# The last layer of a four-layer kernel, rewritten from a loop over batches into a written-out pipeline of three stages

## The reference, cut to what matters

```python
xn = _layernorm(x)
# state-space part (HID 512, 64 heads of width 8, N 128, chunks of Q = 128 tokens)
zxbcdt = xn @ W_in.T                      # z 512, channels 512 + 2*128, steps 64
xBC = causal_conv_silu(zxbcdt[512:1280])  # 4 taps
dt = softplus(dt_raw + dt_bias);  a = dt * -exp(A_log)
# within and across chunks: C_i . B_j * exp(sum of a from j to i) * dt_j, times xs_j
y  = (Yd + Yoff) + D * xs
yz = y * silu(z)
yn = yz * rsqrt(mean(yz*yz) + EPS) * norm_w
x  = x + yn @ W_out.T + (sigmoid(xn @ q(w1).T) * (xn @ q(w2).T)) @ q(w3).T
```

## Time and profile before

| What | Value |
|---|---|
| Median of 3 runs | 1151.38 us |
| Profiled execution, its own time | 1151.5 us |
| Its span, first to last instruction | 1149.7 us |
| PE, DVE, ACT, POOL busy | 969.4, 815.7, 449.7, 463.9 us |
| Mean granted clock of TensorE | 0.928 |
| First instruction of layer 3's norm to the end | 681.4 to 1149.7 us |

### The profile page before, as it was taken

One profiled execution on the slowest core, in us unless ns is written; L12 is line 12 of the kernel. 1 busy time (PEld: TensorE's weight loads), 2 busy tenths in 40 slices (PEclk: granted clock), 3 DMA queues, 4 the chain that ended last, 5 costly groups with the idle time before them and its releaser, 6 DMA issues. The chain is left out here.

```text
span 1149.7 us, 13089 instructions
## 1 busy us (share of the span) xinstructions
PE 969.4 (84%) x4130; PEld 500.7 (44%) x4130; DVE 815.7 (71%) x1432; ACT 449.7 (39%) x732; POOL 463.9 (40%) x480
## 2 busy tenths in 40 slices
PE   3888859979999999579999959888988898889777
PEld 1555535523333333235565545325533553355324
DVE  3667655578888786447768737796679767967795
ACT  1111124427766666257536424311442134224421
POOL 2111047555444442025426420681068206910681
PEclk9999979969999999779999978899889988998899
DMA  8500006322222210020000010000000000000000
GB/s 299 181 14 14 14 0 167 109 64 57 57 67 60 70 30 1 25 107 14 1 15 15 1 39 1 1 1 1 18 0 0 0 18 0 0 9 9 0 0 18
DMA packets 28635, 42.95 MB, mean 37 GB/s; under 512 B 6480, under 2 KB 21792, under 8 KB 28192
## 3 DMA queue, kind: packets, MB, share of 16 engines
q1 hardware_dynamic: 28592, 42.41, 11.9%
HBM read 30.93 MB, written 11.27 MB: 37 GB/s over the span
## 5 line engine op out<-in xcount | busy, mean ns | idle before, releaser
L991 DVE TENSOR_REDUCE l_nmax<-banks 128x1 f32<-128x512 f32 (+1 forms) x165 | 147.9, 930 | 35.0 <-PE banks L1094 34.1
L2328 PE MATMUL banks<-l_scaled,l_cbm 128*128 128x512 f32 x224 | 126.9, 687 | 44.1 <-POOL l_scaled L2038 21.2
L950 ACT ACTIVATE l1b_PT<-banks 128x512 f32<-128x512 f32 (+1 forms) x176 | 134.1, 793 | 67.0 <-PE banks L1107 66.6
L2038 POOL TENSOR_TENSOR l_scaled<-l_X,l_source 128x512 f32<-128x512 f32 x112 | 132.6, 1210 | 0.0
L2207 DVE TENSOR_TENSOR banks<-banks,l_decay 128x512 f32<-128x512 f32 x128 | 87.9, 689 | 18.0 <-PE banks L2328 11.0
L2328 PEld LDWEIGHTS banks<-l_scaled,l_cbm 128*128 128x128 f32 x224 | 41.8, 210 | 116.2 <-POOL l_scaled L2038 76.1
L1094 PE MATMUL banks<-l_KQ 96*128 96x512 bf16 x240 | 82.0, 395 | 7.9 <-DVE l_nmax L991 5.0
L1107 PE MATMUL banks<-l_KQ 99*128 99x512 bf16 x256 | 85.7, 388 | 2.8 <-ACT l1b_PT L950 2.1
L2181 DVE TENSOR_TENSOR l_y<-l_y,banks 128x512 f32<-128x512 f32 x128 | 86.5, 676 | 1.9
L2107 ACT ACTIVATE l_hhi<-l_h 128x512 f16<-128x512 f32 (+1 forms) x24 | 15.1, 630 | 144.5 <-DVE l_h L2220 144.5
L1121 PE MATMUL banks<-l1b_PT,l1b_V 128*32 128x512 f32 x512 | 68.2, 605 | 0.0
(11 more groups left out here) (326 smaller groups left out, 2083.6 us busy)
## 6 DMA issues: line engine op xcount, KB each, us to landing
l_split<-l1a_parts SPq DMA_DIRECT2D x16, 384.0 KB, 3.7
l_KQ<-l_split SPq DMA_DIRECT2D x48, 128.0 KB, 2.9
l_KQ<-l_split SPq DMA_DIRECT2D x16, 192.0 KB, 3.0
l_KQ<-l_split SPq DMA_DIRECT2D x48, 64.0 KB, 2.9
w_ternary<-l_tern_out SPq DMA_DIRECT2D x7, 384.0 KB, 2.3
x<-in_x SPq DMA_DIRECT2D x4, 512.0 KB, 9.5
l_raw<-in_w_gate_up SPq DMA_DIRECT2D x2, 1024.0 KB, 10.0
out<-x SPq DMA_DIRECT2D x4, 512.0 KB, 3.0
```

What stands on the lines that cost most here:

```text
L950: nc.scalar.activation(PT[:, first:first + size, :], source, ACT.Exp, scale=SCALE).then_inc(p_ready, 1)
L991: nc.vector.tensor_reduce(nmax[:, H % 2, first:first + size], source, axis=AX.X, op=ALU.max, negate=True).then_inc(smax_read, 1)
L2038: nc.gpsimd.tensor_tensor(by_head(scaled[:, n % 4, :]), by_head(X[:, T, :]), spread(source[:, level, T, :]), ALU.mult).then_inc(scaled_rea ...
L2328: last = nc.tensor.matmul(bank, cbm[:, T % 2, level, :], scaled[:, own_n % 4, :], start=True, stop=True)
```

## The change

Layer 3 is written out for stages b = -1 to 4. In stage b, the 16 units (pairs of tiles, 1,024 columns each) of batch b's products run; at fixed places beside them stand the beginning of batch b + 1 and the projections of batch b - 1. Units 0 to 6 are the levels of tiles 0 and 1, unit 7 is L128, unit 8 is L256, units 9 to 15 are the levels of tiles 2 and 3. A unit is two matmuls into a pair of banks (4,5 or 6,7); banks 0 and 1 serve the feed-forward and the projections, banks 2 and 3 all the rest. `X`, `decay` and `y` get two buffers, `scaled` goes from four of 512 to two of 1,024 columns.

On single parts: dt is multiplied into X once (`start`), in place of the product of decay and dt (L2170). The diagonal of the state product comes from a product of two channel groups on POOL and four matmuls with a column of ones (`sum_states`), in place of L2195 and L2197. The masks of tiles 0 and 1 read PSUM. Normalisation of the input moves from DVE to ACT; y is normalised on ACT before it is turned, so the two output projections accumulate in one bank and two adds into x become one. In layer 1, a memset on POOL moves from ahead of the first inversion to behind the second.

```diff
-            nc.gpsimd.memset(early.KQ[ROWS:ROWS + PARTS, KEY, :, :, :], 1.0).then_inc(early.ones_set, 1)
-            pool.wait_ge(early.ones_set, 1)
             invert(0)
             for b in range(B):
                 add_bias(b)
                 if b + 1 < B:
                     invert(b + 1)
+                if b == 0:
+                    pool.wait_ge(rstd_ready, 2)
+                    nc.gpsimd.memset(early.KQ[ROWS:ROWS + PARTS, KEY, :, :, :], 1.0).then_inc(early.ones_set, 1)
+                    pool.wait_ge(early.ones_set, 1)
...
+            def start(b, half):
...
+                nc.gpsimd.tensor_tensor(by_head(y[:, b % 2, mine, :]), by_head(X[:, b % 2, mine, :]), spread(coef[:, mine, :]),
+                                        ALU.mult).then_inc(y_started, 1)
+                pool.wait_ge(y_started, b * 2 + half + 1)
+                nc.gpsimd.tensor_tensor(by_head(X[:, b % 2, mine, :]), by_head(X[:, b % 2, mine, :]), spread(dt[:, mine, :]),
+                                        ALU.mult).then_inc(xdt_ready, 1)
+
+            def scale(b, n):
...
+                if q >= 2:
+                    pool.wait_ge(prod_made, own_unit(q - 2) + 1)
+                nc.gpsimd.tensor_tensor(by_head(scaled[:, n % 2, :, :]), by_head(X[:, b % 2, mine, :]),
+                                        spread(decay[:, b % 2, level, mine, :]), ALU.mult).then_inc(scaled_ready, 1)
+
+            def scale_across(b, i):
+                pool.wait_ge(xdt_ready, b * 2 + 2)
+                if b:
+                    pool.wait_ge(post_made, b * 2)
...
+                    for n in range(OWN):
+                        scale(b, n)
+                        if n == 2:
+                            rest_of_input(b)
+                        if n == 3 and b:
+                            invert_rms(b - 1)
+                        if n == 5:
+                            scale_across(b, 0)
+                        if n == 6:
+                            scale_across(b, 1)
...
+                        if n == 12 and b + 1 < B:
+                            multiply_states(b + 1)
...
+                if b + 1 < B:
+                    start(b + 1, 0)
+                    start(b + 1, 1)
...
+                for s in range(4, 12):
+                    if ahead and s - 4 < XBC:
+                        take_channels(b + 1, s - 4)
+                    if now and s >= 6:
+                        round_gated(b, s - 6)
+                    if now and 5 <= s < 11:
+                        gate_sigmoid(b, s - 5)
+                    if now and s == 9:
+                        square_tile(b, 0)
+                        square_tile(b, 1)
+                if ahead:
+                    for i in range(CHUNKS):
+                        decays(b + 1, i)
+                    gate_channels(b + 1)
+                    for t in range(TT):
+                        copy_tokens(b + 1, t)
...
+                for u in range(UNITS):
+                    if now:
+                        apply_decay(b, u)
+                    if now and u:
+                        add(b, u - 1)
+                    elif behind and u == 0:
+                        add(b - 1, UNITS - 1)
+                    if behind and u == 0:
+                        gate_y(b - 1, 1)
+                    if u == 1 and behind:
+                        mean_square(b - 1)
+                    if u == 2 and ahead:
+                        copy_turned(b + 1)
+                    if u == 3:
+                        if now:
+                            mask_late(b, 2)
+                            mask_late(b, 3)
+                        if ahead:
+                            take_steps(b + 1)
+                    if u == 4:
+                        if ahead:
+                            softplus(b + 1)
+                        if behind:
+                            add_x(b - 1, 0)
+                    if u == 5 and behind:
+                        add_x(b - 1, 1)
+                    if 5 <= u < 5 + XBC:
+                        if ahead:
+                            convolve(b + 1, u - 5)
+                        if now:
+                            multiply_gate(b, u - 5)
+                    if now and u == ACROSS_128 + 1:
+                        gate_y(b, 0)
...
+                    if u == 12 and ahead:
+                        weigh_skip(b + 1)
+                    if u == 15 and ahead:
+                        mask(b + 1, 0)
+                        mask(b + 1, 1)
...
+            def feed_forward(b, j):
                 rows = P if j < FT - 1 else LAST
-                if j >= 2:
-                    pe.wait_ge(h_ready, b * FT + (j - 1))
+                if j == 0:
+                    pe.wait_ge(split, b + 1)
+                    pe.wait_ge(up_loaded, 16)
+                    if b:
+                        pe.wait_ge(x_done, b * 2)
+                else:
+                    pe.wait_ge(h_ready, b * FT + j)
...
+            def product(b, u):
+                g = b * UNITS + u
+                if g >= 2:
+                    pe.wait_ge(prod_added, g - 1)
+                bank = unit_bank(u)
...
+                    pe.wait_ge(scaled_ready, b * OWN + n + 1)
+                    for i in range(2):
+                        last = nc.tensor.matmul(ps[bank + i][:, :], cbm[:, 2 * (n // LEVELS) + i, n % LEVELS, :],
+                                                scaled[:, n % 2, i, :], start=True, stop=True)
...
+                for u in range(UNITS):
+                    if now:
+                        product(b, u)
+                    if now and u < 2:
+                        gates(b, 2 * u)
+                        gates(b, 2 * u + 1)
+                    if u == 2:
+                        if now:
+                            late_states(b)
+                        if ahead:
+                            turn_input(b + 1)
+                    if u == 3:
+                        if behind:
+                            turn_y(b - 1)
+                        if ahead:
+                            steps(b + 1)
+                    if behind and u in (3, 4):
+                        project(b - 1, u - 3)
+                    if now and 5 <= u < 5 + FT:
+                        feed_forward(b, u - 5)
+                    if ahead and 4 <= u < 4 + XBC:
+                        channels(b + 1, u - 4)
+                    if ahead and u == 9:
+                        sums(b + 1, 0)
+                        sums(b + 1, 1)
+                    if ahead and u == 11:
+                        for i in range(2, CHUNKS):
+                            sums(b + 1, i)
+                    if ahead and u == 12:
+                        sum_states(b + 1)
+                        turn_tokens(b + 1, 0)
+                    if ahead and u == 13:
+                        for t in range(1, TT):
+                            turn_tokens(b + 1, t)
+                    if ahead and u == 14:
+                        states(b + 1, 0)
+                        states(b + 1, 1)
```

More of the change, by code:

```diff
@@ L2045, in _ @@
+            invert_rms(B - 1)
         @block.scalar
@@ new lines, in channels @@
+            def channels(b, i):
+                if i == 0 and b >= 2:
+                    pe.wait_ge(yt_ready, (b - 2) * NT + 4)
+                elif i == 1:
+                    pe.wait_ge(dt_read, b + 1)
+                elif i > 1:
+                    pe.wait_ge(c_read, b * XBC + i - 1)
+                first = X0 + CHANNELS[i] * P
+                for c in range(CT):
+                    last = nc.tensor.matmul(ps[C_BANK[i]][:, :], w.inner[:, c, first:first + P], xnT[:, c, :],
+                                            start=(c == 0), stop=(c == CT - 1))
+                last.then_inc(c_made, 1)
@@ L2360, in _ @@
[L2360 to L2366 removed]
+                            nc.tensor.matmul(out, part_[rows, j, t * P:(t + 1) * P], w.down[rows, j, :],
+                                             start=(j == 0 and part_ is hhi), stop=False)
```

714 lines of the change are left out of this document (415 added, 299 removed).

## The result

The changed kernel takes 1257.53 us (median of 4 runs, 1257.09 to 1259.28), the kernel before 1151.26 beside it: ratio 1.0926, 95% interval 1.0907 to 1.0945. I had forecast 1213 with a range up to 1240: the sign was right, the size was not. The profiled execution has a span of 1255.2 us; my sum was 1211.1, so 44 us are to be found.

A forecast was written before the change was run, and what follows sets the result against it. Waits at fixed queue places, no full engine, were taken to bound it: full stage 116 plus 10 for collisions. 684.9 + 53 + 109 + 252 + 86 + 27 + 4 = 1215.9; layer 1's 4.8 off, 1211.1 span, 1213 device time; range 1150 to 1240.

The forecast's parts named there:

- Clock term: PE at 1.2 GHz after gaps in units 11 to 15: 34 us more if all did so; none was taken.
- the drain: Layer 3's end behind stage 3's last product, from D and A through projections to an add: 27 us.
- 86: Stage 3, with no next batch ahead, up to P15: 86 us.
- Collisions: DVE and POOL taking turns at SBUF: 8.2 us in softplus, 2 in units 8 to 10, 10 a full stage.
- Collisions are cheap: Rival: softplus slips past POOL; still slower than before, 1184 us, range 1155 to 1190; chance 0.20.
- Collisions in stage 0: Stage 0, with no projections behind it, was put at 109 us, 100 without collisions.
- Second add into x behind D5: FF 0 waits for DVE's add into x, queued behind D5 and A4: PE idle 4 to 12 us.
- The loop of units 5 to 10: ACT's sigmoid queued behind channels and rounding: 6.7 us a unit, against 5.2 on DVE and 5.1 on PE.
- A unit of 4.35: Least cost of a product unit in us, as P(u+1) waits for A(u-1), which DVE does behind D(u).
- Steps: PE's steps for a batch, priced at 3.1 us.
- Layer 1: Moving the memset shortens the norm: gain 4.8 us, or 2 if it stops another DVE operation.
- PE bounds the stages: Rival: queues absorb the waits, a full stage is near 97 us, the total 1127, faster than before; chance 0.14.

The follow-up runs named there:

- clock_fill: Changed kernel plus matmuls that nothing reads, at five places where PE stands idle in units 11 to 13 and ahead of the next P0: 1239.3 us.
- x_first: Changed kernel with, in DVE's queue of stages 1 to 3, softplus moved to unit 3 and the second add into x ahead of D5 and A4: 1234.0 us.
- own_yt: Changed kernel with the turned y in memory of its own, no longer in `across`, so POOL's scale_across needn't wait for project 1: 1250.2 us.
- softplus_early: Changed kernel with the next batch's softplus moved in DVE's queue from unit 4 to right behind take_steps in unit 3: 1247.2 us.
- add at once: Changed kernel with each unit's add into y right behind its own decay on DVE, no longer behind the next unit's decay: 1240.5 us.
- memset_only: Kernel before with one edit: layer 1's memset on POOL moved behind the second inversion: 1145.6 us, ratio 0.9958.
- all_moves: Changed kernel with the edits of x_first, clock_fill and add at once, and ACT's sigmoid ahead of take_channels in stages 0 to 2: 1189.6 us, ratio 1.0348.
- all_moves_late: all_moves with sum_states and the first turned tokens behind product 13 on PE, and weigh_skip in unit 13 on DVE: 1189.0 us, ratio 1.0306.

## Why the forecast was wrong by 44 us

- **Clock term: the step that failed.** I wrote "I take none, since 10 a stage for collisions is an upper figure", with 34 as the other bound. The collisions came at about their full price and the clock came on top. clock_fill shows 20 us for units 11 to P0 of three stages. The rows show more: FF 0 at 3.3 for 1.7 in stages 1 and 2 (3; x_first, where FF 0 doesn't wait, has it at full clock), P14 and P15 of stage 3 at pitches of 5.5 and 6.2 for 4.4 (3), and the drain, at 0.53 from 1220 to 1240, which may be most of its 4.5. That makes some 30 of the 44, 20 of them shown by filling and the others read from rows; FF 1 and the channels behind it (1.8 in each of stages 1 and 2) come on top, hidden by what was forecast too long. I had the gaps in my own ledger (the exponentials, `sum_states`, the wait ahead of P0) and the earlier trace rows had the same effect once already, 0.53 for 5 us. Where a forecast lists gaps of 3 to 6 us on PE, it has to price what follows them.
- **The rest** is small and spread: 2.8 in each tail at full clock (8), 1.5 in the heads of three stages beyond FF 0, 2.6 ahead of stage 0, 1.4 in stage 3. Of that last, 1.2 is a slip: 38.7 + 3.3 + 43.5 + 1.7 is 87.2, and I wrote 86. The alternation of exponentials and sums was the largest single piece, 2 short a stage.
- **Collisions: right in the full stages.** 8.2 forecast in softplus, 6.6 found (14.2 us for 7.6); 2 in the taps, 2.5 found in unit 10 (4.80 for 2.33). The Trainium skill ("SBUF — State Buffer", Who interferes with whom) says that a DVE instruction with both inputs in SBUF contends with a GpSimd instruction that reads SBUF, and that `tensor_scalar`, with one input, can contend too, in a mode that takes both pairs of ports. The trace agrees with both (taps 4.80 for 2.33; the TENSOR_SCALAR of softplus 1.93 for 0.29), and own_yt prices it. "Collisions are cheap" (0.20) is out.
- **Collisions in stage 0: right by luck.** I took 9 there too, though `scale_across` waits for no projection in that stage. Softplus was stretched by 1.7 only (9.3 us); the two late masks (5.47 us for 2.38) and the size of the steps (1.73 for 0.42), which I hadn't named, made up for it.
- **Second add into x behind D5: right.** FF 0 waited 10.0 us in stages 1 and 2 (4 to 12 forecast) and 3.1 in stage 3 (3.3 forecast). Both halves of it were shown by moving them (softplus_early, x_first).
- **The loop of units 5 to 10: right in kind, 5 us short.** `h` 1 to `h` 4 of stage 1 come at 6.6 to 6.9, behind ACT's order; the first pitch, with PE at half clock in FF 1, is 8.3 and the last, with taps beside POOL, 8.9. Its bound below (DVE with collisions) lay nearer than my 5.2.
- **A unit of 4.35: right as a time, wrong as a bound.** Measured 4.4 in stages 0 to 3; 2.4 with the add at once. It decided nothing in the full stages.
- **Steps** took 1.97 rather than 3.1, the one price that I had too high: the row that I took it from the earlier trace rows ran at a granted clock of 0.71 and then 0.50.
- **Layer 1: right.** 4.8 forecast, 4.8 found in the norm and 5.4 between the medians of memset_only and its neighbour, the norm's last operation back from 4.98 to 0.17.
- **"PE bounds the stages" (0.14) is out,** and not by the queues' order alone: with all the moves stage 1 takes 113.6, still above the 105 at which the forecast would have met the time before. Its row in all_moves, and that of its units 5 to 10:

```profile
845.90:959.50 113.60, 102.38 (x407) 54.37 (x406) 82.87 (x97) 42.69 (x73) 52.43 (x30) 1.00 0.02 5
887.30:928.10 40.80, 37.66 (x123) 16.86 (x122) 38.87 (x37) 14.11 (x26) 19.28 (x12) 1.00 0.00 1
```

The clock is full, and PE's 102.4 holds 14 of matmuls that nothing reads (64 of 0.22). What keeps the stage there, from the starts of D: 16.4 us for units 0 to 2, 25.0 for units 3 and 4 (PE's 13.2 of projections, steps, turned y, channels and two units: PE is busy for 22.9), 40.8 for units 5 to 10 and 31.4 for the tail. In units 5 to 10 DVE is busy for 38.9 of 40.8 us, its stretched operations counted in, and PE for 37.7: once the order is mended, two engines are nearly full there. The tail is a serial chain through ACT, DVE and POOL beside which the products find room but gain no time. all_moves_late speaks for that, as its tails keep their length; by how much they would shrink if the chain began earlier wasn't tried. Nor was the drain's clock.

What is left of the loss stands at the two ends of the pipeline. In the profile of all_moves the stages 0 to 2 take 339 us, 9.5 less than three rounds of before. But from the norm's first statistics to D0 of stage 0, stage 3 and the drain together take 164 us, where before the norm's start and one round took 120: with four batches, a beginning and an end that overlap little cost some 45.

## What to carry to other kernels

Overlapping stages buys time only if the hidden chain is shorter than the work it hides behind: sum the serial chain of each part first, and compare it with the other part's length, not with idle shares. In a queue written by hand, put what others wait for ahead of what you wait for yourself (the add ahead of the next decay, the sigmoid ahead of the copies, the add into x ahead of D5), and test each such swap in a stage where nothing else waits. Price a gap on PE twice: its length, and the work behind it at half clock. Price the filling and emptying of a pipeline too, where it has only four rounds.

## What the runs showed of the hardware

- PE came back at 1.2 GHz (clock 0.50) after waits of 5.90 and 4.49 us, and with bf16 matmuls of 0.22 us in these gaps the same stretch was granted 1.00. The added work of 64 matmuls in each of three tails made the kernel 18 us faster.
- A collision cost DVE about 1.6 us of POOL's 2.0, however short its own operation: one on 256 columns of 0.29 took 1.93, and in the tail one of 4 columns 1.77 for 0.16. POOL lost little (2.14 for 1.97). DVE's decay, which reads a product in PSUM, kept its time beside POOL (all 64 of them between 1.215 and 1.233 us). First the row of 4 columns, from stage 1's tail in the changed kernel, then decay and POOL side by side in own_yt:

```profile
978.45 1.77 DVE L2281 SCALAR_TENSOR_TENSOR l_shift<-l_mv,l_rstd 128x4 f32<-128x4 f32 x1
```

```profile
889.10 1.23 DVE L2358 TENSOR_TENSOR banks<-banks,l_decay 128x1024 f32<-128x1024 f32 x1 [7.50 <-PE banks L2626]
...
889.24 1.97 POOL L2062 TENSOR_TENSOR l_scaled<-l_X,l_decay 128x1024 f32<-128x1024 f32 x1 [9.56 <-PE banks L2626]
```
